# A transformer layer in eight batches: the row maxima of batch 1 move among batch 0's scores

## The chip, the cores and the metric

One core of a Trainium2 chip runs the whole kernel. Time is device time in microseconds of one launch. The engines work through queues of their own and wait for each other by semaphores: PE (TensorE, matmuls), ACT (ScalarE), DVE (VectorE), POOL (GpSimd) and SP (SyncE, whose queue issues the DMA transfers). ScalarE's queue can issue transfers too; in the kernel before only SP's does.

## What is computed

x is 8 x 256 x 256 (batch, token, feature), all in float32. Cut to what matters:

```python
# attention: 16 heads of 16, two query sets that share keys and values
scores = einsum('bhqd,bhkd->bhqk', q, k2) / sqrt(16); causal mask
p = softmax(scores); y = p @ v2
y = y1 - sigmoid(x @ Wlam) * y2
x = layernorm(x + y @ Wo)
# FFN: shared MLP of 1024, a routed MLP of 128 scaled by the top 2 of 8 logits
comb = sum of softmax(top2(x @ router.T))
x = layernorm(x + mlp(x, shared) + mlp(x, routed) * comb)
```

with `mlp(x) = (g * sigmoid(g) * u) @ down.T`, g = x @ gate.T and u = x @ up.T.

## The kernel before

Each batch of 256 tokens passes through four stages, and the stages of neighbouring batches are woven into each other by hand: every engine has its own list of instructions, written out in `iteration(i, ...)`, and an engine takes its list strictly in order.

**Projections.** float32 products are made of three fast passes (`product`, lines 666 to 668) of a high and a low part of each operand. `qk_job(b, n)`, n = 0 to 2, projects q and k of a batch into the PSUM banks ybank (12 matmuls). The result is cut into three bfloat16 parts: ScalarE copies it (`raw_part`, `first_part`), POOL subtracts (`rest_part`, L362), ScalarE copies (`second_part`), POOL subtracts (`third_part`, L388). SP stores the parts in DRAM (`store_part`, L256, nine per batch) and loads them back as stacks in which six products of parts lie on 96 rows (`load_stacks`, L272 and L274, twelve loads per batch; there are two stacks for each of q and k). xT is split by ScalarE (`split_xt`) and POOL (L356).

**Scores, twice.** First 22 units `s_unit(b, u)` (L724, L729) make the scores in the order in which a row maximum can be taken, in a ring of three PSUM banks; DVE reduces each (`row_max`, L1010), and a unit waits until the bank it takes was reduced. `max_job` transposes the maxima (L737), ScalarE and DVE make two bfloat16 rows of them (`max_first`, `max_second`), and SP loads these as two more rows of q's stack (`load_max`, L279). Then eight groups `t_group(b, g)` (L750, L754) make the scores again, transposed and with the maximum subtracted; ScalarE takes the exponentials (`exps`, L512, three per group), POOL masks (`causal`, L407), PE multiplies by v (`pv_group`, L778, two groups later), DVE evacuates (L1031).

**Output.** `y_jobs` (L791) transposes, DVE normalizes (`normalize_y`, L1042 to L1056), `yT_job` (L799) transposes back, `wo_job` projects into ybank, DVE adds the input (L1067) and takes the statistics.

**FFN.** `x1T_job`, router and logits, nine `gu_units` of 12 matmuls each with gate and up of 128 columns in two banks `ff` (ScalarE `gate_tanh` L520 and `h_first`, DVE `mlp_unit`, POOL `h_rests` L397), then the down products two iterations later.

In iteration i PE goes through: the 22 score units of batch i, with `qk_job(i + 1)` behind units 3, 6 and 10, the down products of batch i - 2, x1T, router and logits of batch i - 1 among them; gate/up unit 0; `max_job`; units 1 to 3; then the eight groups with units 4 to 6 among them; `y_jobs` with units 7 and 8; v of the next batch, `yT_job`, the first score unit of the next batch, `wo_job`. In iteration 0 there is no batch before it, so the scores stand alone but for batch 1's projections; in iteration 1 there are no down products yet.

SP's list in the set-up: xT of batch 0, the weights, nine stores, xT of batch 1, twelve stack loads. In an iteration: `load_x(i)`, nine stores of batch i + 1, xT of i + 2, `load_max(i)`, twelve stack loads of i + 1, in iteration 0 the three pieces of w_down.

Of the kernel before, what the change touches and what calls it, by code (L numbers as in the profile page):

```python
# [80 lines left out]
PROJ_CHUNKS = QK_JOBS + 1  # L81

# [15 lines left out]
def build_layer(nc, x, xT, w_proj, w_out, w_gu, w_down, w_router, out):  # L98
    with ExitStack() as ctx:
# [142 lines left out]

        block = ctx.enter_context(nc.Block())
# [3 lines left out]
        def _(sp):  # L247
# [15 lines left out]
            def load_stacks(b):  # L263
                if b >= STACKS:
                    sp.wait_ge(t_full, (b - STACKS + 1) * T_UNITS)
                for p in range(3):
                    sp.wait_ge(parts_stored[p], (b + 1) * (16 * QK_JOBS))
                    for s in range(SLOTS):

                        rows = slice(s, STACK_ROWS, SLOTS)  # L270
                        if Q_PARTS[s] == p:
                            sp.dma_start(q_stacks[b % STACKS][rows, :, :, :], scratch[p, :, :, 0:Q_JOBS, :]).then_inc(stack_loaded, 16)  # L272
                        if K_PARTS[s] == p:
                            sp.dma_start(k_stacks[b % STACKS][rows, :, :, :].rearrange("p r h t -> p r (h t)"), scratch[p, :, :, Q_JOBS, :]).then_inc(stack_loaded, 16)  # L274
# [17 lines left out]
            def iteration(i, has_next=True, has_last=True):  # L292
                load_x(i)
                if has_next:
                    store_parts(i + 1, range(QK_JOBS))
                if i + 2 < B:
                    load_xt(i + 2)
                load_max(i)
                if has_next:
                    load_stacks(i + 1)  # L300
# [29 lines left out]
        def _(pool):  # L330
# [90 lines left out]
            def iteration(i, has_next, has_prev, has_last):  # L421
# [11 lines left out]
                if has_prev:  # L433
                    h_rests(i - 1, range(FF_MAX[-1]))
                causal(i, range(0, 1))
                if has_prev:
                    h_rests(i - 1, FF_MAX[-1:])
                for g in range(1, GROUPS):
# [3 lines left out]
                    if has_prev and g - 1 in FF_SCORES:  # L442
                        n = FF_SCORES[g - 1]
                        h_rests(i - 1, range(n, n + 1))
                if has_prev:
# [24 lines left out]
        def _(act):  # L470
# [30 lines left out]
            def max_first(b):  # L501
# [3 lines left out]
                copy(max_parts[:, 0, :], misc[0:HEADS * Q_TILES, 0:P]).then_inc(max_h_done, 1)  # L505

# [66 lines left out]
            def iteration(i, has_next, has_prev, has_last):  # L573
                if has_next:
                    split_xt(i + 1)
# [11 lines left out]
                if has_prev:  # L587
                    x1T_first(i - 1)
                if has_next:
# [3 lines left out]
                if has_prev:  # L593
# [3 lines left out]
                if has_prev:  # L597
                    router_exp(i - 1)
                    mlp_units(i - 1, (FF_FIRST,))
                max_first(i)  # L600
                if has_prev:
# [3 lines left out]
                exps(i, 0)  # L605
                if has_prev:
                    h_first(i - 1, FF_MAX[-1])
                    gate_tanh(i - 1, FF_SCORES[0])
                for g in range(1, GROUPS):
# [53 lines left out]
        def _(pe):  # L663
# [48 lines left out]
            def s_unit(b, u):  # L712

                if u == 0:
# [6 lines left out]
                bank = ring[u % RING]  # L721
# [18 lines left out]
            def t_group(b, g):  # L740

                rows = slice(0, STACK_ROWS + MAX_PARTS)
                for u in range(3):
                    if g == 0:
# [71 lines left out]
            def x1T_job(b):  # L816
                pe.wait_ge(yT_lo_done, b + 1)
                for t in range(TT):
# [80 lines left out]
            def iteration(i, has_next, has_prev, has_last):  # L899
                if i == 2:  # L900
                    pe.wait_ge(mlp_w_lo_done, W_DOWN)
                if not has_prev:
                    first_scores(i)
                for u in range(S_UNITS):
                    if u > 0:
                        s_unit(i, u)
                    if has_next and u in QK_AT:
# [11 lines left out]
                if has_prev:  # L919
                    gu_units(i - 1, (FF_FIRST,))  # L920
                max_job(i, has_prev)
                if has_prev:
                    gu_units(i - 1, FF_MAX)
                pe.wait_ge(max_loaded, (i + 1) * (16 * MAX_PARTS))
                for g in range(GROUPS + 2):
                    if g < GROUPS:
                        t_group(i, g)
                    if g in FF_SCORES and has_prev:
                        gu_units(i - 1, (FF_SCORES[g],))
                    if g >= 2:  # L930
# [10 lines left out]
                if has_next:  # L941
                    v_job(i + 1, 1)
                    first_scores(i + 1)
                wo_job(i)

# [28 lines left out]
        def _(dve):  # L974
# [32 lines left out]
            def row_max(b, u):  # L1007
                dve.wait_ge(s_full, b * S_UNITS + u + 1)
                i, columns, keys = s_job(u)
                dve.tensor_reduce(neg_max[:, columns.start:columns.stop, i], ring[u % RING][:, 0:len(columns) * keys].rearrange("p (h k) -> p h k", k=keys),  # L1010
# [125 lines left out]
            def iteration(i, has_prev, has_last):  # L1136
# [9 lines left out]
                for u in range(1, S_UNITS):  # L1146
                    row_max(i, u)
                    if has_prev:

                        if u - 2 == X1T_AT:  # L1150
                            x1T_second(i - 1)
                        if u - 1 == LOGIT_AT:
                            router_top(i - 1, router_steps[0])
                if has_prev:
                    mlp_unit(i - 1, FF_FIRST)
                max_second(i)
                attn[0](dve.tensor_scalar(lam[:, :, :], lam_th[:, :, :], 0.5, 0.5, ALU.mult, ALU.add))
                if has_prev:
# [4 lines left out]
                if has_prev:  # L1163
                    mlp_unit(i - 1, FF_SCORES[0])
                for g in range(GROUPS):
                    if g == 0 and is_first(i):
                        dve.wait_ge(mlp_w_lo_done, W_GATE_UP)
                    if has_prev and g + 1 in FF_SCORES:
# [14 lines left out]
                if i + 1 < B:  # L1183
# [75 lines left out]
```

## Time and profile before

| | us |
|---|---|
| median of 3 runs | 481.44 (481.05 to 482.01) |
| the profiled execution | 480.8 |
| its span, first to last instruction | 479.1 |
| PE busy | 420.2 (88%) |
| DVE, ACT, POOL busy | 279.6, 237.2, 243.8 |
| mean granted clock of PE | 0.963 of full |

The profile shows one execution. Times in it count from the first instruction. An engine's busy time says nothing by itself of what it costs: what counts is which engine waits for which at each place. The granted clock has two levels here, 1.00 (2.4 GHz) and 0.50 (1.2 GHz). Matmuls are pipelined, so their starts are better marks than their ends: the distance between two starts is what a piece of PE's work takes.

### The profile page before, as it was taken

How to read it: one execution, taken by the hardware profiler on the slowest of the kernel's cores; microseconds unless marked ns; L12 is line 12 of the kernel's file. 1: busy time of each engine (PE TensorE's matmuls, PEld its weight loads, DVE VectorE, ACT ScalarE, POOL GpSimd, SP SyncE). 2: the span in 40 equal slices, each digit the busy share in tenths (PEclk: the TensorE clock that was granted, in tenths of full speed). 3: DMA queues.
4: the chain of work that ended last, by engine and by line, in shares of the span. 5: the costliest groups of instructions: out<-in, count | busy, mean ns of one | idle time of the engine just before them, and what ended most of it. 6: DMA issues, size and time to landing. Idle time of an engine off the chain costs nothing.

```text
span 479.1 us, 10336 instructions
## 1 busy us (share of the span) xinstructions
PE 420.2 (88%) x4008; PEld 336.0 (70%) x4008; DVE 279.6 (58%) x676; ACT 237.2 (50%) x532; POOL 243.8 (51%) x334
## 2 busy tenths in 40 slices
PE   5129687899999999999999999999999999997995
PEld 4126246775998579875988579866987588855995
DVE  3617237844758366745757476755757378746374
ACT  4604482477254843476254843475355831483140
POOL 8305374556354845567354834566364822383142
PEclk9659699999999999999999999999999999999899
DMA  8762760362023610381024511280034410000000
GB/s 287 233 150 69 201 176 1 113 169 64 1 77 105 142 45 24 99 191 36 23 80 125 118 45 38 87 199 24 23 91 115 98 47 0 4 1 24 1 23 23
DMA packets 34753, 40.41 MB, mean 84 GB/s; under 512 B 4240, under 2 KB 28304, under 8 KB 34448
## 3 DMA queue, kind: packets, MB, share of 16 engines
q1 hardware_dynamic: 34704, 39.75, 30.9%
q8 instruction: 32, 0.52, 0.5%
q14 instruction: 17, 0.14, 0.1%
HBM read 27.94 MB, written 11.53 MB: 82 GB/s over the span
## 4 chain that ended last, share of the span: by engine, by line
PE 66%; DVE 13%; ACT 10%; issue 4%; DMA 3%; SPq 2%; POOL 1%; POOLq 0%; DVEq 0%; ACTq 0%
PE ff L666 10%; PE ff L668 9%; PE ff L667 9%; PE ybank L778 8%; DVE neg_max L1010 7%; ACT prob L512 6%; PE ring L729 5%; PE ring L750 4%; PE ybank L666 4%; PE ybank L667 3%; PE ybank L668 3%; PE ybank L791 3%; PE ring L754 3%; PE ring L724 3%; DMA q_stack<-qk_parts_dram 2%
## 5 line engine op out<-in xcount | busy, mean ns | idle before, releaser
L1010 DVE TENSOR_REDUCE neg_max<-ring 128x2 f32<-128x512 f32 (+3 forms) x176 | 104.2, 636 | 46.2 <-PE ring L729 45.6
L512 ACT ACTIVATE prob<-ring 128x512 f32<-128x512 f32 x192 | 100.3, 620 | 14.7 <-PE ring L750 14.6
L397 POOL TENSOR_TENSOR h_lo<-h_full,h_hi 128x256 fp32r<-128x256 f32 x72 | 52.9, 734 | 100.2 <-ACT h_hi L472 100.2
L407 POOL TENSOR_SCALAR_AFFINE_SELECT prob<-prob 128x512 f32<-128x512 f32 x128 | 83.4, 676 | 23.8 <-ACT prob L512 23.5
L666 PE MATMUL ff<-x1T_hi,wg_lo 128*128 128x256 f32 x288 | 85.8, 298 | 0.1
L667 PE MATMUL ff<-x1T_lo,wg_hi 128*128 128x256 f32 x288 | 80.4, 279 | 0.0
L668 PE MATMUL ff<-x1T_hi,wg_hi 128*128 128x256 f32 x288 | 80.4, 279 | 0.0
L1031 DVE COPY yv<-ybank 128x256 f32<-128x256 f32 x64 | 26.5, 421 | 75.3 <-PE ybank L778 75.3
L520 ACT ACTIVATE gate_t<-ff 128x256 f32<-128x256 f32 x72 | 27.8, 386 | 73.9 <-PE ff L668 72.7
L724 PE MATMUL ring<-mask_b,ident_b 128*128 128x128 bf16 (+2 forms) x176 | 44.6, 254 | 20.6 <-DMA q_stack<-qk_parts_dram 18.4
L729 PE MATMUL ring<-k_stack,q_stack 96*128 96x256 bf16 (+3 forms) x512 | 58.9, 235 | 0.0
L666 PEld LDWEIGHTS ff<-x1T_hi,wg_lo 128*128 128x128 f32 x288 | 54.3, 188 | 3.6 <-DVE h_full L1026 1.9
L778 PE MATMUL ybank<-prob,v_ones 128*32 128x256 f32 (+1 forms) x1024 | 54.9, 336 | 0.1
L667 PEld LDWEIGHTS ff<-x1T_lo,wg_hi 128*128 128x128 f32 x288 | 54.3, 188 | 0.0
L668 PEld LDWEIGHTS ff<-x1T_hi,wg_hi 128*128 128x128 f32 x288 | 54.0, 188 | 0.0
L750 PE MATMUL ring<-q_stack,k_stack 98*128 98x512 bf16 x128 | 41.8, 399 | 7.7 <-ACT prob L512 3.9
L1020 DVE SCALAR_TENSOR_TENSOR gate_t<-gate_t,ff 128x256 f32<-128x256 f32 x72 | 29.9, 415 | 26.3 <-ACT gate_t L520 26.2
L778 PEld LDWEIGHTS ybank<-prob,v_ones 128*32 128x32 f32 x1024 | 26.9, 110 | 24.5 <-DVE yv L1031 5.7
L362 POOL TENSOR_TENSOR rest<-rest,parts 128x512 f32<-128x512 f32 x21 | 24.4, 1161 | 31.5 <-ACT parts L472 31.5
L472 ACT ACTIVATE rest<-ybank 128x512 f32<-128x512 f32 x21 | 12.5, 594 | 53.1 <-PE ybank L668 53.1
L729 PEld LDWEIGHTS ring<-k_stack,q_stack 96*128 96x128 bf16 x512 | 36.6, 100 | 3.0 <-issue 0.6
L666 PE MATMUL ff<-wd_hi,h_lo 128*128 128x256 f32 x124 | 37.7, 304 | 0.0
(164 smaller groups left out, 886.1 us busy)
## 6 DMA issues: line engine op xcount, KB each, us to landing
q_stack<-qk_parts_dram SPq DMA_DIRECT2D x48, 256.0 KB, 4.6
qk_parts_dram<-parts SPq DMA_DIRECT2D x72, 128.0 KB
k_stack<-qk_parts_dram SPq DMA_DIRECT2D x48, 128.0 KB, 4.4
xt_raw<-xT SPq DMA_DIRECT2D x8, 256.0 KB, 2.7
xz<-x SPq DMA_DIRECT2D x8, 256.0 KB, 2.8
out<-xz SPq DMA_DIRECT2D x7, 256.0 KB, 2.2
prob<-w_gu SPq DMA_DIRECT2D x1, 1152.0 KB, 7.8
yv<-w_gu SPq DMA_DIRECT2D x1, 1024.0 KB, 9.5
```

The costliest lines, as they stand in the source:

```text
L397: pool.tensor_tensor(h_lo[:, n, :], h_full[:, n % RING, :], h_hi[:, n, :].bitcast(F32), ALU.subtract).then_inc(h_lo_done, 1)
L407: pool.affine_select(out=v, in_=v, compare_op=ALU.is_ge, fill=0.0, base=0, pattern=[[0, 2], [HALF, 2], [0, 2], [1, HALF]], channel_multipl ...
L512: act.activation(prob[:, g % RING, u, :], ring[u][:, :], ACT.Exp, scale=SCALE).then_inc(exp_done, 1)
L666: pe.matmul(o, lhs_lo, rhs_hi, start=first, stop=False)
L667: pe.matmul(o, lhs_hi, rhs_lo, start=False, stop=False)
L668: return pe.matmul(o, lhs_hi, rhs_hi, start=False, stop=last)
L724: pe.matmul(o[:, :, keys - HALF:keys], ident_b[:, :], mask_b[:, :].unsqueeze(1).to_broadcast([P, len(columns), HALF]), start=True, stop=Fa ...
L729: mm = pe.matmul(o[:, j, :], q_stacks[b % STACKS][rows, row, block, i * P:(i + 1) * P], k_stacks[b % STACKS][rows, row, block, 0:keys], st ...
L750: mm = pe.matmul(ring[u][:, :], keys_of(b, rows, n, slice(0, P)), q_pair(b, rows, n, slice(0, 2 * T)), start=True, stop=True)
L778: mm = pe.matmul(bank[V_COLS * j:V_COLS * (j + 1), t * P:T], v_ones[:, t, 2 * g + j // 2, :], p, start=(t == 0), stop=(t == TT - 1))
L1010: dve.tensor_reduce(neg_max[:, columns.start:columns.stop, i], ring[u % RING][:, 0:len(columns) * keys].rearrange("p (h k) -> p h k", k=keys),
L1020: dve.scalar_tensor_tensor(gate_t[:, n % RING, :], gate_t[:, n % RING, :], 1.0, ff[n % 2][:, 0:T], ALU.add, ALU.mult).then_inc(gate_done, 1)
```

## The change

Batch 1 is singled out (`EARLY = 1`).

- Set-up: xT of batch 1 is loaded and split ahead of the stores and of the other weights' splits. ScalarE's queue issues the six stack loads of part 0 of batch 0 behind the values' copies, SP's the other six.
- Iteration 0: PE does the three `qk_job` of batch 1 ahead of batch 0's score units and none among them. SP waits for batch 0's stacks before it stores batch 1's parts. The two rows of batch 0's maxima are loaded by ScalarE's queue (`load_first_max`). From step 2 of the group loop on, three score units of batch 1 stand in each step behind `t_group` and ahead of `pv_group`, in the two banks `ff` in place of the ring, and DVE reduces them there; `max_job(1)` follows `wo_job(0)`.
- Iteration 1: PE begins with the three `qk_job` of batch 2, then goes to the groups. x1T, router, logits and gate/up units 0 to 6 of batch 0 stand in steps 1, 2, 3 and 3 to 9. ScalarE's first instruction is `max_first(1)`, ahead of the split of xT; SP loads the maxima ahead of the stores. POOL's masks come ahead of batch 0's `h_rests`.

The diff, cut to its core:

```diff
+EARLY = 1
+EARLY_FROM, EARLY_STEP = 2, 3
+EARLY_X1T, EARLY_ROUTER, EARLY_LOGIT = 1, 2, 3
...
+        def s_bank(b, u):
+            return ff[u % 2] if b == EARLY else ring[u % RING]
+        def early_units(step):
+            first = max(step - EARLY_FROM, 0) * EARLY_STEP
+            return range(first, min(first + EARLY_STEP, S_UNITS) if step >= EARLY_FROM else first)
...  SP, iteration
+                if i == EARLY:
+                    load_max(i)
+                if is_first(i):
+                    sp.wait_ge(stack_loaded, 16 * STACK_LOADS)
                 if has_next:
                     store_parts(i + 1, range(QK_JOBS))
...
-                load_max(i)
+                if i not in (0, EARLY):
+                    load_max(i)
...  SP, set-up
+            load_xt(1)
             for n, p in ((0, 0), (1, 0), (0, 1), (2, 0), (1, 1), (2, 1), (0, 2), (1, 2), (2, 2)):
                 store_part(0, n, p)
-            load_xt(1)
-            load_stacks(0)
+            load_stacks(0, range(1, 3))
...  ScalarE, set-up
             for t in range(TT):
                 values(0, t)
+            load_part(act, 0, 0)
+            split_xt(1)
             split_weight(wo_hi[:, :, :], wo_raw, wo_loaded)
...  ScalarE, iteration
+                if i == EARLY:
+                    max_first(i)
                 if has_next:
-                    split_xt(i + 1)
+                    if has_prev:
+                        split_xt(i + 1)
                     raw_part(i + 1, 0)
...
+                if is_first(i):
+                    load_first_max()
...
+                if i == EARLY:
+                    for step in range(1, GROUPS + 2):
+                        if step < GROUPS:
+                            exps(i, step)
+                        if step == EARLY_X1T:
+                            x1T_first(i - 1)
+                        if step == EARLY_ROUTER:
+                            router(i - 1)
+                        if step >= EARLY_LOGIT:
+                            gate_tanh(i - 1, step - EARLY_LOGIT)
+                        if step == EARLY_LOGIT:
+                            router_exp(i - 1)
+                        if step > EARLY_LOGIT:
+                            h_first(i - 1, step - EARLY_LOGIT - 1)
...  PE, s_unit
+                if b == EARLY:
+                    if u > 1:
+                        pe.wait_ge(max_done, b * S_UNITS + u - 1)
...  PE, iteration
                 if not has_prev:
+                    for n in range(QK_JOBS):
+                        qk_job(i + 1, n)
                     first_scores(i)
+                if i == EARLY:
+                    for n in range(QK_JOBS):
+                        qk_job(i + 1, n)
...
                     if g < GROUPS:
                         t_group(i, g)
+                    if i == EARLY:
+                        if g == EARLY_X1T:
+                            x1T_job(i - 1)
+                        if g == EARLY_ROUTER:
+                            router_job(i - 1)
+                        if g == EARLY_LOGIT:
+                            logit_job(i - 1)
+                        if g >= EARLY_LOGIT:
+                            gu_units(i - 1, (g - EARLY_LOGIT,))
...
+                    if i + 1 == EARLY:
+                        if g == EARLY_FROM:
+                            first_scores(i + 1)
+                        for u in early_units(g):
+                            if u > 0:
+                                s_unit(i + 1, u)
                     if g >= 2:
                         pv_group(i, g - 2, has_next)
...
                 wo_job(i)
+                if i + 1 == EARLY:
+                    max_job(i + 1, False)
...  DVE, iteration
                 for g in range(GROUPS):
+                    if i == EARLY:
+                        step = g + 2
+                        if step == EARLY_ROUTER:
+                            x1T_second(i - 1)
+                        if step == EARLY_LOGIT:
+                            router_top(i - 1, router_steps[0])
+                        if step >= EARLY_LOGIT:
+                            mlp_unit(i - 1, step - EARLY_LOGIT)
+                        if step == EARLY_LOGIT + 1:
+                            router_sum(i - 1, *router_steps)
+                    if i + 1 == EARLY:
+                        for u in early_units(g + 2):
+                            row_max(i + 1, u)
...
                     evacuate_pv(i, g)
```

## Rows read from the trace of the kernel before

**Rows 1.** The page's slices: busy tenths of TensorE (PE) in 40 slices.

```profile
PE   5129687899999999999999999999999999997995
```

**Rows 2.** SP's queue in order of time: start us, us, engine line, transfer, count.

```profile
9.23 8.27 SPq L256 DMA_DIRECT2D qk_parts_dram<-parts  x9
...
18.07 0.64 SPq L272 DMA_DIRECT2D q_stack<-qk_parts_dram  x1
...
25.16 0.60 SPq L272 DMA_DIRECT2D q_stack<-qk_parts_dram  x1
...
50.35 1.16 SPq L279 DMA_DIRECT2D q_stack<-max_parts  x2
```

**Rows 3.** Line 272 (stack loads), 0 to 70 us: from issue to landing.

```profile
DMA to landing us min/median/max: 3.4/5.0/7.6
```

**Rows 4.** Line 279 (the maxima's two rows), whole span: from issue to landing.

```profile
DMA to landing us min/median/max: 2.1/2.1/2.2
```

**Rows 5.** Windows: stretch, length, engines' busy time, granted clock, DMA share, GB/s.

```profile
24.00:26.00 2.00, 0.00 (x0) 0.00 (x0) 0.00 (x0) 0.00 (x0) 1.14 (x1) 0.50 1.07 237
...
50.00:52.00 2.00, 0.01 (x1) 0.00 (x0) 0.37 (x2) 0.27 (x1) 0.00 (x0) 0.69 0.65 197
...
61.00:62.00 1.00, 1.00 (x16) 0.43 (x8) 0.42 (x1) 0.30 (x2) 1.00 (x2) 1.00 1.14 264
```

**Rows 6.** Groups of instructions, 33 to 50 us, DVE: busy us, mean ns, idle before.

```profile
L1010 DVE TENSOR_REDUCE neg_max<-ring 128x2 f32<-128x384 f32 (+3 forms) x22 | 12.6, 636 | 13.3 <-PE ring L729 13.3
```

**Rows 7.** PE in order of time, columns as in rows 2, idle before in brackets.

```profile
53.12 1.04 PE L750 MATMUL ring<-q_stack,k_stack 98*128 98x512 bf16 x2 [3.11 <-DMA q_stack<-max_parts]
...
69.46 1.34 PE L791 MATMUL ybank<-ident,yv 128*128 128x128 f32 x8
...
80.89 0.37 PE L666 MATMUL ybank<-xt_hi,wp_lo 128*128 128x256 f32 x1
...
85.23 0.23 PE L724 MATMUL ring<-mask_b,ident_b 128*128 128x128 bf16 x1
...
86.28 0.23 PE L724 MATMUL ring<-mask_b,ident_b 128*128 128x128 bf16 x1 [0.20 <-DVE neg_max L1010]
...
101.57 0.36 PE L666 MATMUL ff<-x1T_hi,wg_lo 128*128 128x256 f32 x1
...
103.07 0.60 PE L750 MATMUL ring<-q_stack,k_stack 98*128 98x512 bf16 x2
...
107.17 0.86 PE L778 MATMUL ybank<-prob,v_ones 128*32 128x256 f32 x16
107.96 0.60 PE L750 MATMUL ring<-q_stack,k_stack 98*128 98x512 bf16 x2
...
108.71 0.86 PE L778 MATMUL ybank<-prob,v_ones 128*32 128x256 f32 x16
...
120.16 0.36 PE L666 MATMUL ff<-x1T_hi,wg_lo 128*128 128x256 f32 x1
```

**Rows 8.** ScalarE (ACT) in order of time.

```profile
61.82 6.35 ACT L512 ACTIVATE prob<-ring 128x512 f32<-128x512 f32 x12 [0.70 <-PE ring L750]
...
82.61 0.60 ACT L472 ACTIVATE rest<-ybank 128x512 f32<-128x512 f32 x1 [3.97 <-PE ybank L668]
...
89.61 0.60 ACT L472 ACTIVATE x1T_hi<-misc 128x512 fp32r<-128x512 f32 x1
```

**Rows 9.** GpSimd (POOL) in order of time.

```profile
72.56 1.85 POOL L392 TENSOR_TENSOR wd_lo<-h_full,wd_hi 128x768 fp32r<-128x768 f32 x1
78.72 1.29 POOL L356 TENSOR_TENSOR xt_lo<-xt_raw,xt_hi 128x512 fp32r<-128x512 f32 x1 [4.31 <-ACT xt_hi L472]
```

**Rows 10.** VectorE (DVE) in order of time.

```profile
71.13 1.50 DVE L1046 TENSOR_TENSOR recip<-recip,lam 128x16 f32<-128x16 f32 x1
...
79.98 0.69 DVE L1067 TENSOR_TENSOR xz<-ybank,xz 128x512 f32<-128x512 f32 x1 [1.15 <-PE ybank L668]
...
120.73 0.17 DVE L1046 TENSOR_TENSOR recip<-recip,lam 128x16 f32<-128x16 f32 x1
```

More of the change, by code:

```diff
@@ L241, in qk_bank, with load_part @@
             return (ybank[0], ybank[1], misc if is_first(b) else ybank[0])[n]
+        def load_part(queue, b, p):
+            queue.wait_ge(parts_stored[p], (b + 1) * (16 * QK_JOBS))
+            for s in range(SLOTS):
+                rows = slice(s, STACK_ROWS, SLOTS)
+                if Q_PARTS[s] == p:
+                    queue.dma_start(q_stacks[b % STACKS][rows, :, :, :], scratch[p, :, :, 0:Q_JOBS, :]).then_inc(stack_loaded, 16)
+                if K_PARTS[s] == p:
+                    queue.dma_start(k_stacks[b % STACKS][rows, :, :, :].rearrange("p r h t -> p r (h t)"), scratch[p, :, :, Q_JOBS, :]).then_inc(stack_loaded, 16)
+        def s_bank(b, u):
[3 more added lines that the diff above has]
+            return range(first, min(first + EARLY_STEP, S_UNITS) if step >= EARLY_FROM else first)
         block = ctx.enter_context(nc.Block())
@@ L261, in store_parts, with load_stacks @@
                         store_part(b, n, p)
-            def load_stacks(b):
+            def load_stacks(b, parts):
                 if b >= STACKS:
                     sp.wait_ge(t_full, (b - STACKS + 1) * T_UNITS)
[L266 to L274, printed above, removed]
+                for p in parts:
+                    load_part(sp, b, p)
             def load_max(b):
@@ L604, in iteration @@
                     act.wait_ge(mlp_w_lo_done, 1)
-                exps(i, 0)
-                if has_prev:
+                if i == EARLY:
[12 more added lines that the diff above has]
+                            h_first(i - 1, step - EARLY_LOGIT - 1)
+                    h_first(i - 1, FF_Y0 - 1)
+                else:
+                    exps(i, 0)
+                if has_prev and i != EARLY:
                     h_first(i - 1, FF_MAX[-1])
                     gate_tanh(i - 1, FF_SCORES[0])
-                for g in range(1, GROUPS):
+                for g in range(1, GROUPS if i != EARLY else 1):
                     exps(i, g)
@@ L902, in iteration @@
                 if not has_prev:
+                    for n in range(QK_JOBS):
+                        qk_job(i + 1, n)
                     first_scores(i)
[L904 removed]
+                if i == EARLY:
+                    for n in range(QK_JOBS):
+                        qk_job(i + 1, n)
+                for u in range(S_UNITS if i != EARLY else 0):
                     if u > 0:
                         s_unit(i, u)
[L907 removed]
+                    if has_next and has_prev and u in QK_AT:
                         qk_job(i + 1, QK_AT.index(u))
@@ L1009, in row_max @@
                 i, columns, keys = s_job(u)
-                dve.tensor_reduce(neg_max[:, columns.start:columns.stop, i], ring[u % RING][:, 0:len(columns) * keys].rearrange("p (h k) -> p h k", k=keys),
+                dve.tensor_reduce(neg_max[:, columns.start:columns.stop, i], s_bank(b, u)[:, 0:len(columns) * keys].rearrange("p (h k) -> p h k", k=keys),
                                   AX_X, ALU.max,
```

86 lines of the change are left out of this document (57 added, 29 removed).

## Prediction

> **What bounds the kernel now.** I read the page's slices first, then the chain of waits, then the windows and the order of time of each engine over the first 130 us. TensorE (PE) works in nine tenths or more of most slices after the first six [rows 1]: from batch 2 on it is the bound, and what the change can gain lies before. There PE waits for others four times. (a) It stands still until 32.87 us for the q and k stacks of batch 0: SP's queue stores the parts, then issues twelve loads from 18.07 us, the last at 25.16 us [rows 2], and that one lands after 7.6 us [rows 3]; while it does, the DMA engines are full (share 1.07) and PE's granted clock is 0.50, its lower level of 1.2 GHz [rows 5]. (b) Batch 0's scores for the maxima need 22 reductions on VectorE (DVE), 12.6 us of work [rows 6]; with projections between them the stage lasts from 32.87 to about 49.7 us. (c) The maxima's own rows take 2.1 us to land [rows 4], PE waits 3.11 us for them [rows 7], and the clock falls to 0.50 again, not to rise before 61 us [rows 5]. (d) Batch 1's scores for the maxima run from 79.8 to 96 us, again at DVE's pace, with projections, x1T, router and the first gate/up unit between them. W below is the end of batch 0's output projection, 79.8 us (DVE's addition follows at 79.98 [rows 10]).
>
> **The start.** ScalarE's queue now issues six of the twelve loads. At 0.64 us each (twelve from 18.07 to 25.8 us [rows 2]) that moves SP's last issue from 25.2 to about 20.8 us; batch 1's xT load leaves the place ahead of it as well. Bounds for the last landing: issue plus the median 5.0 us, 25.8 us; or no gain from the second queue at all, since the engines are already full at 24 us, and only the xT load is saved, 32 us. Twelve loads are 2.36 MB, at the 237 GB/s of that window 10 us, and they can't start before the third of the first parts is stored (the fourth of nine stores that run from 9.23 to 17.5 us [rows 2], behind the weights; I estimate 16 to 16.5 us), and bytes flow some 2 us later (the 2.1 us of the smallest load [rows 4]). I take 29.4 us, nearer to 20.8 + 7.6 = 28.4 than to 32. That is -3.5 us. The Trainium skill (DMA: Bandwidth & Descriptors, section "Issuing engines are not separate DMA queues") says that a second issuing engine saves only the issuing time, as all end on the same 16 DMA engines; the full share in the row agrees, and by it alone the gain would be nearer the small bound. ScalarE pays for it: six issues, 3.8 us if they cost what SP's do, bounds 0 and 7. Behind them stand the split of batch 1's xT and those of the weights, 5.1 us in a row, so batch 1's first copy comes at about 25.5 to 26.5 us. PE does batch 1's three projections, about 1.5 us each at 2.4 GHz (twice that at 1.2), while it would wait anyway; the third may end at 28 us, or 29.4 at the lower clock. That cover is full: nothing added.
>
> **Batch 0's scores (b).** Without projections between them the stage is DVE's 12.6 us plus 0.6 us in front, 13.2 instead of 16.8 us: -3.6, together -7.1 us.
>
> **Its maxima (c).** They go out on ScalarE's queue, because SP's is full: it now waits for batch 0's stacks, stores batch 1's parts (the chain of copies and subtractions took 10.5 us before, so it ends near 37 us) and then issues the twelve loads of batch 1, 37 to 45 us, landing by about 50. So the two small rows, at 43 us, travel beside full engines, which no row shows; alone they land in 2.1 us [rows 4], loads in such a crowd in up to 7.6 us [rows 3]. I take 3.1: they are small and on a queue of their own. +1.0 us, at most +5.5. The same page ("Queues, rings and completion order") says that a DMA engine takes turns between queues, packet by packet; by that the delay would be near 0 and the sum 1 us lower; no row here has two queues. T(0), the stage of batch 0's own scores (L750, L754) and their products with v (L778), starts at 47.0 instead of 53.12 us.
>
> **T(0) with batch 1's maxima in it.** Now 53.12 to 69.46 us, 16.3 us [rows 7]. In each of eight steps PE gets three more score units, in the two FFN banks. With two banks the third unit has to wait until DVE has reduced the first. Rows: with three banks, a unit at 85.23 us frees its bank for the one at 86.28 [rows 7], so 1.05 us from a unit to the next of its bank, for 384 columns; for 512 the reduction is 0.16 us longer. With the third unit's own 0.24 to 0.33 us a triple takes about 1.3 (three of them) or 1.55 us (four), and the last step has one unit, 0.3: 10.4 us. Scores of a group take 0.75 us, products 0.79 [rows 7]. The first three groups take 4.4 us, as now. T(0) = 4.4 + 10.4 + 5 x 0.75 + 8 x 0.79 = 24.9 us. The clock: now it is back 7.9 us after T(0)'s start; in the stretch from 4.4 to 7.9 us PE's own work is at half speed, +1.4 us (0 if it never falls). So 26.3 us, +9.9 us. ScalarE (three exponentials, 1.6 us a step [rows 8]), DVE (2.3) and POOL (1.3) stay under PE's 3.0 us. Batch 1's stacks are needed after the third group, 51.4 us; they land at about 50.
>
> **To W.** VectorE's L1046 took 1.50 us at 71.13 us, 0.17 us in the next batch, and waited until POOL's splits of w_down were through [rows 9, 10]. With T(0) longer, ScalarE's exponentials end 5 us before PE's last products, and those splits end at about 1.2 us behind T(0), before L1046 (1.7 us behind it). Saved: about 1.8 us (bounds 0 and 2.2). W is at -7.1 + 1.0 + 9.9 - 1.8 = +2.0 us.
>
> **From W to batch 0's gate/up unit 7** (120.16 us now, W + 40.4 [rows 7]). The 16 us stage (d) is gone, but what stood beside it isn't, and now has no cover. ScalarE first waits for the transposed maxima (W + 0.6), then splits xT of batch 2 (before W until now), POOL subtracts, 1.3 us [rows 9], and PE's projection starts at W + 2.6. 1.7 us later comes the first copy, and the copies and subtractions take 7.0 us until ScalarE is free (82.61 to 89.61 us [rows 8]): exponentials of batch 1 start only at W + 11.35, though its maxima have landed at W + 4.6. PE is idle for about 4 us. Then exponentials (1.6), a copy (0.55), exponentials (1.6), x1T's two parts and hand-overs (1.5): W + 16.4; router 0.7, products 0.8: W + 17.9. Steps 3 to 7 are PE's: 0.75 + 1.5 (a gate/up unit, 101.57 to 103.07 us [rows 7]) + 0.79 = 3.04, with 0.2 for the logits 15.4: W + 33.3. Two steps without scores, 4.6: W + 37.9. DVE does unit 6 ahead of the last evacuation, so the second transposes end at W + 39.6. Idle for 4 us, PE loses its clock before the exponentials, as it did behind (b): half speed costs the router and the first products 0.7 + 0.8 us, of which I take 1.2 (bounds 0 and 3). 40.8 against 40.4: +0.4 us. Behind that nothing is changed and PE is the bound.
>
> **The sum**, against the profiled execution's own 480.8 us: -3.5 - 3.6 + 1.0 + 9.9 - 1.8 + 0.4 = +2.4, 483.2 us. The median of the runs lies 0.6 us above that execution: 483.8 us.
>
> **Rivals.** (1) The long stages pack better: loads land at 28 us (-1.4), the small rows lose nothing (-1.0), the clock holds in T(0) and behind W (-2.6), triples overlap more than the bank rule says (-1.5). Together -6.5 at most, any half of it is -3.2: 477.3 to 480.5 us, typically 479.5. For it: PE is idle less than before in the first 45 us, and busy early. (2) Slower by a wait for batch 1's stacks. PE takes its queue in order, so if they land after the third group (51.4 us; my margin is 1.4 us) scores, products and exponentials all stand. Landing at 7.6 us from the last issue, with ScalarE's six issues at 1.2 us instead of 0.64: 45.5 + 3.4 + 7.6 = 56.5 us, +5 us: 489 us. It decides from 51.4 us on. For it: the engines are full in each burst of loads; against: in the second burst the median was under 5 us. (3) It doesn't do what it says at the start: transfers and not issues are the bound, S(0) begins at 32 us: +2.6, 486.5 us. (4) The two changes in T(0) and behind W are dearer than thought, DVE's reductions lagging: +3, 487 us.
>
> **Chances.** Forecast 0.45 (481 to 486), rival 1 0.28, rival 2 0.11, rival 3 0.08, rival 4 0.08. A measurement of this kernel can tell about 0.2%, 1 us. Faster than 480.5 us: rival 1 and a little of the forecast's lower end, 0.30; within: 0.20; slower: 0.50. The range, 477.5 to 489 us, leaves out a tenth on each side.
>
> **What would show it.** First score unit (L724) at 29.4 us; the 22 reductions without a gap over 0.2 us and the transposed maxima at 42.6 us; the small rows' landing under 3.5 us; T(0) of 26 us with PE waiting for neg_max once in each step; L1046 at 0.2 us; exponentials of batch 1 at W + 11; PE idle for 4 us ahead of them with a clock of 0.50. Wrong would be a wait of PE for q_stack in T(0), steps of 2.5 us or less, or exponentials of batch 1 at W + 5.

## The result, and the profile after

The changed kernel takes 488.51 us (median of 4 runs, 486.60 to 491.42), the one before 481.50 us (4 runs on the same chip): 1.6% slower, ratio 1.016, 95% interval 1.0135 to 1.0184. The forecast was 483.8 us, slower by 2.4 us; it is slower by 7.0 us. The profiled execution is the fastest of the four: 486.6 us, its span 484.8 us. Medians below are of all runs of a kernel, but the ratios leave out runs over 1.5% above its fastest (four of e4's ten, five of e8's).

First the page of the changed kernel: busy tenths of PE, its granted clock and the DMA engines' share, in 40 slices of 12.1 us.

```profile
PE   4285787689999999999999999999999999999895
...
PEclk9785599879999999999999999999999999999998
DMA  8778700175003700254112810362122610000000
```

In the first ten slices, where the kernel before had 5129687899 [rows 1], PE's digits have only moved: the third is 8 in place of 2, the fourth 5 in place of 9, and both rows add up to 64. The clock has a second dip at the eighth and ninth slices, around 97 us, where there was none.

PE in order of time in the changed kernel, at the marks that the prediction named: start us, us, engine line, operation, out<-in, shape and count; in brackets PE's idle time before it, and what ended it.

```profile
31.68 0.39 PE L784 MATMUL ring<-mask_b,ident_b 128*128 128x512 bf16 x1 [1.42 <-DMA q_stack<-qk_parts_dram]
...
44.58 0.42 PE L797 MATMUL misc<-ident,neg_max 128*64 128x128 f32 x1 [1.07 <-DVE neg_max L1101]
51.42 1.03 PE L815 MATMUL ring<-q_stack,k_stack 98*128 98x512 bf16 x2 [6.42 <-DMA q_stack<-max_parts]
...
61.19 0.28 PE L784 MATMUL ff<-mask_b,ident_b 128*128 128x256 bf16 x1 [0.45 <-DVE neg_max L1101]
...
77.56 1.33 PE L856 MATMUL ybank<-ident,yv 128*128 128x128 f32 x8
...
86.03 0.27 PE L797 MATMUL misc<-ident,neg_max 128*64 128x128 f32 x1
88.57 0.36 PE L723 MATMUL ybank<-xt_hi,wp_lo 128*128 128x256 f32 x1 [2.27 <-POOL xt_lo L376]
...
98.42 0.88 PE L815 MATMUL ring<-q_stack,k_stack 98*128 98x512 bf16 x2 [3.17 <-ACT prob L543]
...
127.57 0.36 PE L723 MATMUL ff<-x1T_hi,wg_lo 128*128 128x256 f32 x1
```

They answer to [rows 7], and give the sum term by term (us; "before" from [rows 7] and the first waits told there):

| stage | before | forecast | after |
|---|---|---|---|
| first score unit of batch 0 (L784, before L724) | 32.87 | 29.4 | 31.68 |
| scores for the maxima, to their transposition | 16.84 | 13.2 | 12.90 |
| from there to T(0), the rows of maxima | 3.41 | 4.4 | 6.84 |
| T(0) | 16.34 | 26.3 | 26.14 |
| from T(0) to W | 10.33 | 8.5 | 8.47 |
| from W to gate/up unit 7 of batch 0 | 40.37 | 40.8 | 41.54 |
| gate/up unit 7 | 120.16 | 122.6 | 127.57 |

W is 86.03 us, where the transposed maxima of batch 1 follow the output projection. Of the 7.4 us at unit 7, 5.7 are left at the end of the span. The stretch from 440 to 450 us in the kernel before, then in the changed one (length, busy time of PE, PE's weight loads, DVE, ACT, POOL, then granted clock, DMA share, GB/s):

```profile
440.00:450.00 10.00, 7.98 (x54) 7.56 (x53) 3.75 (x10) 2.68 (x6) 2.73 (x6) 0.83 0.00 0
440.00:450.00 10.00, 7.52 (x89) 6.06 (x82) 7.79 (x22) 2.53 (x7) 2.78 (x5) 1.00 0.09 29
```

The traces of all kernels here are of one of these two kinds. From unit 7 to the end they take either 357.2 to 357.5 us, with a clock of 1.00 from 430 to 460 us (changed, e1, e3, e10, e12), or 358.8 to 359.2 us, with a fall of the clock in that stretch (before, e2, e4, e5, e6, e8, e9, e11). One trace each doesn't show what decides between them, but a single traced execution can differ from another by these 1.7 us behind everything that the change touches.

The DMA side, in three views of the changed kernel. ScalarE's queue and ScalarE in order of time:

```profile
17.83 0.64 ACTq L254 DMA_DIRECT2D q_stack<-qk_parts_dram  x1
...
45.34 1.17 ACTq L536 DMA_DIRECT2D q_stack<-max_parts  x2
...
97.77 1.57 ACT L543 ACTIVATE prob<-ring 128x512 f32<-128x512 f32 x3
```

The two rows of maxima (line 536), from issue to landing:

```profile
DMA to landing us min/median/max: 5.1/5.3/5.5
```

And windows, as in [rows 5]: stretch, length, busy time of PE, PE's weight loads, DVE, ACT, POOL, then granted clock, DMA share, GB/s.

```profile
26.00:28.00 2.00, 2.00 (x11) 2.00 (x11) 2.00 (x2) 2.00 (x4) 0.00 (x0) 0.50 1.08 234
46.00:48.00 2.00, 0.00 (x0) 0.00 (x0) 0.00 (x0) 0.00 (x0) 0.00 (x0) 0.50 1.13 241
90.00:92.00 2.00, 2.00 (x11) 2.00 (x11) 0.00 (x0) 1.08 (x2) 0.09 (x1) 0.50 0.00 0
96.00:98.00 2.00, 0.00 (x0) 0.00 (x0) 0.00 (x0) 1.72 (x4) 1.20 (x2) 1.00 0.42 128
...
104.00:106.00 2.00, 2.00 (x19) 0.81 (x19) 0.12 (x1) 0.37 (x1) 1.06 (x2) 0.50 1.03 268
108.00:110.00 2.00, 2.00 (x26) 1.26 (x25) 0.75 (x2) 0.57 (x3) 0.85 (x2) 1.00 1.13 240
```

ScalarE's loads begin at 17.83 us, when the first parts have landed. From 22 to 30 us the DMA engines are full (1.08 at 26 us), as before the change [rows 5]: the same loads take the same time, whoever issues them. And at 46 us, while the rows of maxima travel, the engines are full again with batch 1's stack loads (1.13): the rows need 5.3 us in place of 2.1 [rows 4], and PE does nothing. The last four windows are for the clock, below: behind W it is 0.50 twice, from about 89.5 to 93 us, behind the wait of 2.27 us at 88.57 us, and from about 100 to 106.5 us.

### The profile page after: what moved, and what is told of

It is laid out like the page before. It is cut to its first block, busy times and chain, and to the rows that moved or that the text cites. A ratio compares the mean times of both kernels' runs of the same rounds, so it can differ in the third digit from the quotient of the medians.

```text
span 484.8 us, 10334 instructions
## 1 busy us (share of the span) xinstructions
PE 425.0 (88%) x4008; PEld 338.9 (70%) x4008; DVE 279.7 (58%) x676; ACT 237.6 (49%) x532; POOL 245.6 (51%) x334
## 4 chain that ended last, share of the span: by engine, by line
PE 64%; DVE 14%; ACT 11%; DMA 5%; issue 4%; POOL 2%; SPq 0%; POOLq 0%; ACTq 0%; DVEq 0%
PE ff L723 10%; PE ff L725 9%; PE ff L724 9%; DVE neg_max L1101 8%; ACT prob L543 7%; PE ybank L843 7%; PE ring L789 4%; PE ring L815 4%; PE ybank L723 3%; PE ybank L856 3%; PE ybank L724 3%; PE ybank L725 3%; PE ring L819 3%; PE ring L784 2%; DMA q_stack<-qk_parts_dram 2%
## 5 line engine op out<-in xcount | busy, mean ns | idle before, releaser
L1101 DVE TENSOR_REDUCE neg_max<-ring 128x2 f32<-128x384 f32 (+3 forms) x154 | 91.0, 636 | 32.2 <-PE ring L789 31.7
L724 PE MATMUL ff<-x1T_lo,wg_hi 128*128 128x256 f32 x288 | 80.2, 278 | 0.0
L724 PEld LDWEIGHTS ff<-x1T_lo,wg_hi 128*128 128x128 f32 x288 | 54.3, 188 | 0.0
L789 PE MATMUL ring<-k_stack,q_stack 96*128 96x64 bf16 (+3 forms) x448 | 52.8, 238 | 0.0
L723 PE MATMUL ybank<-xt_hi,wp_lo 128*128 128x256 f32 x92 | 30.0, 326 | 17.3 <-issue 8.5
L784 PE MATMUL ring<-mask_b,ident_b 128*128 128x128 bf16 (+2 forms) x154 | 39.1, 254 | 2.6 <-DMA q_stack<-qk_parts_dram 1.4
L408 POOL TENSOR_TENSOR parts<-rest,parts 128x512 bf16<-128x512 f32 x24 | 27.8, 1162 | 19.6 <-ACT parts L498 11.6
L382 POOL TENSOR_TENSOR rest<-rest,parts 128x512 f32<-128x512 f32 x21 | 25.8, 1230 | 23.2 <-ACT parts L498 23.2
```

What stands on the lines that cost most here:

```text
L723: pe.matmul(o, lhs_lo, rhs_hi, start=first, stop=False)
L724: pe.matmul(o, lhs_hi, rhs_lo, start=False, stop=False)
L784: pe.matmul(o[:, :, keys - HALF:keys], ident_b[:, :], mask_b[:, :].unsqueeze(1).to_broadcast([P, len(columns), HALF]), start=True, stop=Fa ...
L789: mm = pe.matmul(o[:, j, :], q_stacks[b % STACKS][rows, row, block, i * P:(i + 1) * P], k_stacks[b % STACKS][rows, row, block, 0:keys], st ...
```

## The experiments

e1 to e12 differ from the changed kernel or from an earlier experiment by the edit shown, in diffs cut to their core. Times are medians; each ratio is to the kernel before, run in turns on the same chip, with its 95% interval. The stages are read from the profile of each kernel as in the table above.

### e1: not woven

```diff
-EARLY = 1
+EARLY = -1
```

> The changed kernel with EARLY = -1: batch 1's maxima and its gate/up units stand where they stood before the change; the rest of the change stays (six stack loads on ScalarE's queue, batch 1's xT and projections early, batch 0's maxima rows on ScalarE's queue). My theory: weaving batch 1's scores into T(0) costs more than the stage behind W gives back, because PE was nearly full in that stage (3.8 of 4 us from 80 to 88 us). Before, the scores cost nothing there; woven, T(0) takes 26.1 instead of 16.3 us, and W to gate/up unit 7 takes 41.5 instead of 40.4 us. So without the weaving T(0) starts near 51.4 us as in the changed kernel, takes 16.3 us again, and the kernel is about 1.5 us faster than before the change, 480 us. Rival: the start is at fault (ScalarE's issues, late rows) and the weaving pays; then this kernel stays slow, 484 us or more.

Measured: 478.14 us, ratio 0.9941 (0.9919 to 0.9963). PE in e1, in order of time:

```profile
51.91 1.03 PE L815 MATMUL ring<-q_stack,k_stack 98*128 98x512 bf16 x2 [7.06 <-DMA q_stack<-max_parts]
...
67.97 1.34 PE L856 MATMUL ybank<-ident,yv 128*128 128x128 f32 x8
```

T(0) is 16.06 us again, and W to unit 7 is 40.37 us, as before. So the rest of the change gains 2.7 us (the kernel before took 480.86 us in the same turns), and the weaving costs some 10 us (0.9941 against 1.016, 2.2%). The rows of maxima are late here too (PE waits 7.06 us). The profiled execution is the slowest of e1's ten (479.75 us), and its way from T(0) to W is 12.16 us, with a clock of 0.50 from about 73 to 80 us; in e11, whose code is the same there, it is 10.33 us at 1.00. So in this trace nothing is gained yet at unit 7 (120.50 us), and the changed kernel is only 7.1 us behind it there; in e11 unit 7 starts at 114.80 us, 5.4 us ahead of the kernel before.

### e2: the rows of maxima ahead of batch 1's stack loads

e1, with this edit:

```diff
-                if i not in (0, EARLY):
+                if i != EARLY:
                     load_max(i)
...
-                if is_first(i):
-                    load_first_max()
```

> As e1, and batch 0's two rows of maxima are issued by SP's queue again, ahead of the twelve stack loads of batch 1, which so begin some 5 us later. My theory: the rows landed 5.3 us from their issue instead of 2.1 because the DMA engines were full of batch 1's stack loads. Here they land in 2.1 to 2.2 us, T(0) starts 3 us earlier than in e1 (48.2 us), and the kernel takes 477 us. Rival: ScalarE's queue itself is slow, or the delay has another cause (the core's clock, the rows' place): then either the landing stays at 5 us or the time doesn't follow, 480 us.

Measured: 475.37 us, ratio 0.9874 (0.9833 to 0.9915). PE in e2:

```profile
48.31 1.03 PE L813 MATMUL ring<-q_stack,k_stack 98*128 98x512 bf16 x2 [3.09 <-DMA q_stack<-max_parts]
...
63.97 1.33 PE L854 MATMUL ybank<-ident,yv 128*128 128x128 f32 x8
```

and its line 294, all sixteen rows of maxima, from issue to landing:

```profile
DMA to landing us min/median/max: 2.1/2.1/2.1
```

The rows land in 2.1 us and T(0) starts 3.6 us earlier than in e1, at 48.31 us; the time follows by 2.8 us.

### e3: batch 1's stack loads wait for the rows

The changed kernel, woven (as e4 and e5 are), with this edit:

```diff
+                if is_first(i):
+                    sp.wait_ge(max_loaded, 16 * MAX_PARTS)
                 if has_next:
                     load_stacks(i + 1, range(3))
```

> The changed kernel; SP's queue holds the twelve stack loads of batch 1 back until batch 0's rows of maxima have landed. The rows stay on ScalarE's queue. If crowding is the cause, they land in 2.1 us and T(0) starts at 48 us; if ScalarE's queue is the cause, 5 us as before. The stacks then come too late for the first woven score unit: loads from 48 to 56 us, landing at 60 to 62 us, so PE waits some 8 us for q_stack in T(0), and the kernel takes about 491 us.

Measured: 492.58 us, one run. Line 538, the rows on ScalarE's queue, from issue to landing, and then the waits of PE for DMAs from 48 to 70 us:

```profile
DMA to landing us min/median/max: 2.1/2.1/2.2
```

```profile
48.77 1.04 PE L817 MATMUL ring<-q_stack,k_stack 98*128 98x512 bf16 x2 [3.12 <-DMA q_stack<-max_parts]
61.19 0.61 PE L786 MATMUL ff<-mask_b,ident_b 128*128 128x512 bf16 x1 [8.01 <-DMA q_stack<-qk_parts_dram]
```

ScalarE's queue isn't slow: with nearly empty DMA engines (share 0.02 from 44 to 50 us) it delivers in 2.1 us. It is the crowd. The second line shows what rival 2 of the prediction would have been: 8.0 us of PE's time, when the woven units stand in its queue ahead of their stacks. In the changed kernel itself no such wait was there (T(0) went on at 55.6 us without one), so rival 2 didn't come.

### e4: three banks

```diff
-                    if u > 1:
-                        pe.wait_ge(max_done, b * S_UNITS + u - 1)
+                    if u > 2:
+                        pe.wait_ge(max_done, b * S_UNITS + u - 2)
...
-            return ff[u % 2] if b == EARLY else ring[u % RING]
+            return (ff[0], ff[1], misc)[u % 3] if b == EARLY else ring[u % RING]
```

> The changed kernel with three PSUM banks for batch 1's woven score units instead of two. My theory: in seven steps PE waits 0.43 to 0.51 us for the reduction of the first unit of the triple, because the third takes its bank. With a third bank that wait goes, and the first unit of the next step has been reduced long ago: T(0) 22.8 to 23.2 us instead of 26.1, the kernel about 3 us faster than the changed one. Rival: DVE or ScalarE becomes the bound of a step; then T(0) stays over 25 us.

Measured: 486.99 us (ten runs, 480.76 to 489.18), ratio 1.0083 (1.0044 to 1.0122). PE in e4:

```profile
50.49 1.03 PE L815 MATMUL ring<-q_stack,k_stack 98*128 98x512 bf16 x2 [5.61 <-DMA q_stack<-max_parts]
...
72.94 0.63 PE L856 MATMUL ybank<-ident,yv 128*128 128x128 f32 x4
```

T(0) is 22.45 us: 3.7 us shorter than the changed kernel's 26.14, so the waits for the bank are real. But the kernel gains little: its median lies 6.1 us above the kernel before in the same turns, the changed one's 7.0. In the traced run the way to W takes 0.8 us more (9.28), and from W (82.2 us) to unit 7 it takes 44.5 us instead of 41.5. Windows of e4 behind its W:

```profile
92.00:94.00 2.00, 0.00 (x0) 0.00 (x0) 0.00 (x0) 1.51 (x4) 1.20 (x3) 1.00 0.39 104
96.00:98.00 2.00, 2.00 (x9) 1.19 (x8) 0.00 (x0) 2.00 (x5) 1.20 (x2) 0.50 0.43 131
...
102.00:104.00 2.00, 2.00 (x16) 0.63 (x8) 0.42 (x1) 0.70 (x2) 0.00 (x0) 0.50 0.93 235
106.00:108.00 2.00, 2.00 (x15) 1.39 (x17) 0.26 (x1) 0.48 (x2) 0.00 (x0) 0.50 1.09 269
```

PE's clock is 0.50 from about 95 to 108.5 us, twice as long as in the changed kernel (about 100 to 106.5 us), and falls at the end of a wait of 3.9 us. Both have the earlier fall too (here from 85 to 88 us, behind the wait for the split of xT). In this run most of the gain in T(0) went into the longer second fall.

### e5: batch 2's xT split ahead of the copy of the maxima

```diff
-                if i == EARLY:
-                    max_first(i)
                 if has_next:
                     if has_prev:
                         split_xt(i + 1)
+                    if i == EARLY:
+                        max_first(i)
```

> The changed kernel; in iteration 1 ScalarE splits batch 2's xT ahead of the copy of batch 1's transposed maxima, while it idles behind the values' copies. My theory: behind W the chain maxima copy, xT split, POOL's subtraction sets when batch 2's first projection starts (2.6 us behind W), and with it all copies ahead of batch 1's exponentials. Now the split is done 2 us earlier, the projection starts 0.9 us behind W when the addition is through, and W to gate/up unit 7 falls from 41.5 to 39.9 us: the kernel 1.6 us faster than the changed one, 487 us. Rival: the maxima's landing sets the stage; then nothing is gained.

Measured: 487.49 us (four runs, 483.82 to 489.52), ratio 1.0114 (1.0056 to 1.0172). W to unit 7 is 39.18 us, 2.4 less than in the changed kernel. Batch 2's first projection starts at W + 1.0 instead of W + 2.5, the first fall of the clock is gone (1.00 until 97 us), batch 1's exponentials start at W + 9.7 instead of W + 11.7, and PE's clock is back at 1.00 at about 104.5 us, W + 17.8, where the changed kernel's is at about 106.5 us, W + 20.5. So the order on ScalarE is late by what was expected of it or a little more, since the clock changes too; the two aren't told apart here. The whole kernel's 1.0 us is less than its own scatter.

### e8: three banks, and the gap filled

e4, with this edit:

```diff
+            def filler(n):
+                for h in range(2):
+                    f = slice((2 * n + h) * P, (2 * n + h + 1) * P)
+                    for k in range(DK):
+                        product(ff[1][:, h * T:(h + 1) * T], wp_hi[:, k, f], wp_lo[:, k, f],
+                                xt_hi[:, k, :], xt_lo[:, k, :], k == 0, k == DK - 1)
...
                     if i == EARLY:
+                        if g == 0:
+                            for n in range(2):
+                                filler(n)
```

> As e4 (three banks), with two projection-sized jobs of 12 matmuls each, whose results nobody reads, on PE behind batch 1's first group of scores, in a bank that is free: 3 us of work in a gap in which PE waited 3.9 us for batch 1's first exponentials. My theory: e4's gain in T(0), 3.7 us, is given back behind W because PE's clock falls to half in and behind that gap (from 94.8 to 108.4 us in e4's trace), not because of the wait itself. With the gap filled the clock stays up, W to gate/up unit 7 takes 40 us instead of 44.5, the kernel takes 483 us, and its runs scatter less than e4's 8 us. Rival: the late exponentials cost the time; then extra work on PE changes nothing or costs up to 1 us.

Measured: 487.07 us (ten runs, 480.33 to 489.54), ratio 1.0047 (1.0002 to 1.0092); W to unit 7 44.51 us in the profiled execution, which is the slowest of the ten (489.54 us). A miss: neither the median nor the scatter changed. Windows of e8:

```profile
94.00:96.00 2.00, 2.00 (x19) 1.95 (x17) 0.00 (x0) 1.49 (x4) 1.19 (x2) 1.00 0.41 128
96.00:98.00 2.00, 1.07 (x6) 0.32 (x5) 0.00 (x0) 1.98 (x5) 1.79 (x2) 1.00 0.41 121
98.00:100.00 2.00, 1.50 (x9) 0.68 (x8) 0.00 (x0) 2.00 (x5) 1.40 (x2) 1.00 0.46 137
100.00:102.00 2.00, 1.13 (x5) 0.88 (x6) 0.69 (x1) 1.87 (x4) 2.00 (x4) 0.67 0.51 137
102.00:104.00 2.00, 2.00 (x20) 1.15 (x19) 0.00 (x0) 0.37 (x1) 1.53 (x3) 0.50 1.02 300
...
106.00:108.00 2.00, 2.00 (x9) 2.00 (x10) 0.64 (x3) 0.44 (x1) 1.30 (x2) 0.50 1.09 237
```

The gap is full (PE busy 2.00 of 2 us at 94 us), yet the clock falls in the window of 100 us, behind 4.5 us in which PE is busy for half to three quarters of the time and never idle for 1 us on end. "The idle gap drops the clock" was too simple. The runs of e8 also differ: the two fastest (480.33 and 480.62 us) have a mean granted clock of 0.972 over the whole kernel, the five slowest 0.949 to 0.952.

### e9: woven, all three mends

e8 with e5's order on ScalarE.

> The woven kernel with all three mends: three banks, the gap filled, the xT split early. If weaving is a loss in itself, because PE had little to gain in the stage that it empties, this is still slower than the same kernel not woven (e1, 478.1 us): T(0) 22.5 instead of 16.3 us, W to gate/up unit 7 38.5 instead of 40.4 us, so 4 us above e1, 482 us. Rival: with the mends the weaving pays, and the time is under 478 us.

Measured: 484.24 us (ten runs, 480.85 to 486.61), ratio 1.0050 (1.0017 to 1.0082). T(0) 22.51, W to unit 7 41.50 us: 3 us more than expected, again with a clock of 0.50 for ten us. As expected it is slower than e1. Windows of e9:

```profile
92.00:94.00 2.00, 0.97 (x4) 0.37 (x5) 0.00 (x0) 1.99 (x5) 1.73 (x2) 1.00 0.40 117
94.00:96.00 2.00, 1.61 (x9) 0.70 (x8) 0.00 (x0) 2.00 (x5) 1.46 (x2) 0.82 0.46 137
96.00:98.00 2.00, 1.35 (x7) 0.90 (x7) 0.69 (x1) 1.81 (x4) 2.00 (x4) 0.50 0.53 144
```

This execution (484.72 us) is in the middle of its ten, and the fall at 95.4 us follows a thinly filled stretch as in e8; ahead of it lies one wait of 1.30 us.

### e10: the thin stretch filled too

e9, with this edit:

```diff
                         if g == EARLY_X1T:
                             x1T_job(i - 1)
+                            filler(0)
                         if g == EARLY_ROUTER:
+                            filler(1, 1)
                             router_job(i - 1)
```

The second number is how many of the two halves are done.

> As e9, with more unread matmuls: twelve behind x1T's transposes and six ahead of the router. In e8's trace the gap ahead of the exponentials was filled (PE waited 0.7 instead of 3.9 us), and the clock fell all the same, at 100.9 us, in the stretch that follows, where PE waits for exponentials and x1T and is busy for 0.3 to 0.9 of each us. So my theory changes: the thinly filled stretch from W + 11 to W + 17 lets the clock fall, not the gap alone. With that stretch filled too the clock stays at 1.00 until the gate/up units, W to gate/up unit 7 takes 38.5 to 39 us instead of e9's 41.5, and the kernel takes 481.5 us. Rival: the clock isn't what costs; then nothing changes or the extra work adds up to 1 us. In either case a kernel that stays above e1 (478.1 us), though its clock holds, shows that the weaving is a loss in itself.

Measured: 481.78 us (ten runs, 480.79 to 483.42), ratio 1.0026 (1.0009 to 1.0042). Windows of e10, W at 84.7 us:

```profile
92.00:94.00 2.00, 1.79 (x16) 1.58 (x14) 0.00 (x0) 1.49 (x4) 1.19 (x2) 1.00 0.42 121
94.00:96.00 2.00, 0.78 (x2) 0.19 (x2) 0.00 (x0) 2.00 (x5) 1.98 (x2) 1.00 0.43 133
96.00:98.00 2.00, 1.94 (x17) 1.93 (x18) 0.00 (x0) 1.99 (x6) 1.21 (x2) 1.00 0.45 136
98.00:100.00 2.00, 2.00 (x17) 1.71 (x16) 0.69 (x1) 2.00 (x5) 2.00 (x4) 1.00 0.43 114
100.00:102.00 2.00, 2.00 (x26) 1.05 (x24) 0.43 (x1) 0.99 (x3) 1.74 (x3) 1.00 0.96 296
102.00:104.00 2.00, 2.00 (x22) 1.76 (x26) 0.41 (x3) 1.31 (x4) 1.30 (x2) 1.00 0.91 242
104.00:106.00 2.00, 2.00 (x28) 1.47 (x21) 1.18 (x3) 1.37 (x5) 0.00 (x1) 1.00 1.04 238
```

The clock stays at 1.00, W to unit 7 is 37.88 us, the shortest of all, and the runs scatter by 2.6 us where e4's and e8's scattered by 8 and 9 and e9's by 5.8. PE's wait of 1.30 us is there as in e9; what differs is the stretch behind it. Eighteen matmuls more than in e9 (42 in all), whose results nobody reads, save 3.6 us against its 41.5. So the clock is what costs behind W in the traced runs. That it makes the scatter is likely but not shown run by run: e10's ten (480.79 to 483.42) lie where the fastest of e4, e8 and e9 do (480.76, 480.33, 480.85), so the filling makes no fast run faster, it takes the long ones away. For the kernel as a whole the gain over e9 is not clear of noise, as the intervals of the ratios overlap.

### e11 and e12: who issues batch 0's stack loads

e11 is e2 again. e12 (first run as e6) is e2 with all twelve loads on SP's queue:

```diff
-            load_part(act, 0, 0)
...
-            load_stacks(0, range(1, 3))
+            load_stacks(0, range(3))
```

> As e2 (not woven, the rows ahead of the stack loads), with all twelve stack loads of batch 0 issued by SP's queue again; batch 1's xT and projections stay early. My first theory was that issuing is the bound of the start; the trace of the changed kernel shows full DMA engines from 22 to 30 us and a first score unit at 31.7 us, so now I expect transfers to be the bound: the first unit moves by 0.7 us at most (32.5 us) and the kernel takes 475.4 to 476.2 us. Rival (issuing is the bound): the first unit at 34 us or later, 478 us.

> e2 again, in more rounds and on the same chip as e12: 475.4 us, a ratio of 0.987 to the kernel before. It tells, with e12, whether six loads on ScalarE's queue gain anything.

> e6 again. If transfers are the bound of the start, it agrees with e11 within 1 us; if issuing were, it would be 2 us slower or more.

Measured: e6 476.94 us, ratio 0.9889 (0.9842 to 0.9936); then, six runs each on one chip, e11 475.17 us, 0.9878 (0.9857 to 0.9899), and e12 475.36 us, 0.9887 (0.9863 to 0.9911). The first score unit in e11 and in e12:

```profile
31.67 0.39 PE L782 MATMUL ring<-mask_b,ident_b 128*128 128x512 bf16 x1 [1.25 <-DMA q_stack<-qk_parts_dram]
```

```profile
31.32 0.61 PE L781 MATMUL ring<-mask_b,ident_b 128*128 128x512 bf16 x1 [6.42 <-DMA q_stack<-qk_parts_dram]
```

Six loads on a second queue gain nothing: the first unit comes even 0.35 us earlier with all of them on SP's. But PE waits 6.42 us there, as batch 1's projections are through earlier, and the scores begin at a clock of 0.50: they take 13.73 instead of 12.91 us, and T(0) starts at 48.56 against 47.96 us. The two kernels end within 0.2 us of each other. e11 is also the version to keep: it is 1.2% faster than the kernel before and 2.7% faster than the changed one.

## Why the prediction was wrong, point by point

**Direction, and most terms, right.** Four of six terms came within 0.7 us: batch 0's scores without projections (12.90, forecast 13.2 us), T(0) with the woven units (26.14, 26.3 us), the way to W with POOL's splits out of the way (8.47, 8.5 us; L1137, before L1046, took 0.17 us), W to unit 7 (41.54, 40.8 us). The bank rule's waits are in the trace, 0.43 to 0.51 us in six steps. That the stage behind W would give back nothing was the argument that the change is slower; e1 bears it out. (The sum behind W has a slip: its terms to the router add up to W + 16.6, not W + 16.4.)

**The start was mis-sized: 1.2 us instead of 3.5.** I put the first unit at 29.4 us, near the bound that comes from issuing. The row with a DMA share of 1.07 stood in my own groups; by it the bound was 32 us, and rival 3 was the case. The rule of the Trainium skill that I set aside (DMA: Bandwidth & Descriptors, "Issuing engines are not separate DMA queues") is borne out by e11 against e12: no difference. What the start does gain, it gains by the earlier xT and projections, not by the second queue.

**The rows of maxima were mis-sized: +3.4 us instead of +1.0.** The bounds 0 and 5.5 were right, the choice between them was not. "Small, and on a queue of their own" was no argument from a row. e2 and e3 take the crowd away, on either queue, and the rows land in 2.1 us again. The same page's rule that a DMA engine takes turns between the queues packet by packet ("Queues, rings and completion order") was read as a delay near 0; measured were 3.8 to 6.1 us to land, in the woven kernels and in e1, so that reading fails here, and the measurement decides. Why the rows were held up, by turns or otherwise, isn't shown.

**The clock behind W** was taken as 1.2 us, for one fall ahead of the exponentials. In the profiled execution the stage came out 0.7 us over the forecast, but the mechanism was in part another: the gap was there (3.17 us, exponentials at W + 11.7), the clock fell only behind it, at about 99.7 us, and an earlier fall, behind the wait of 2.27 us after W, was not foreseen. That the total agrees is partly luck. It isn't one value either: W to unit 7 was 41.5, 41.5 and 44.5 us in the changed kernel, e3 and e4, which have the same order of work there, and 37.9 with the clock held (e10, with e5's order). The median lies 1.9 us above the profiled execution, the fastest run of four. A fall of the clock in the stretch from 440 to 450 us, which the profiled execution was spared, would account for 1.7 of them; the recorded mean clocks of the other three runs (0.953 to 0.956 against 0.955) don't decide it, and only one run has a trace.

The sum: 2.4 forecast + 2.3 (start) - 0.3 + 2.4 (rows) - 0.2 + 0.7 = 7.3 us at unit 7; measured 7.4. The start and the rows of maxima are 4.7 us of the 5.0 that were missing: these two terms failed, and both for the same reason, the full DMA engines.

**What the weaving costs.** T(0), the way to W and W to unit 7 together: before 67.0 us, changed 76.2, e10 70.4 (e11, not woven, 66.8). Even with a third bank, the better order and the clock held, it is 3.4 us more than before: T(0) takes 6.9 us more, and what follows gives back only 3.5. The unread matmuls stand behind W, so the 6.9 us are free of them; whether they cost something of what is given back isn't shown. The stage that the weaving empties, in windows of the kernel before:

```profile
80.00:84.00 4.00, 3.85 (x46) 3.40 (x45) 3.93 (x9) 1.08 (x2) 1.46 (x6) 1.00 0.00 0
84.00:88.00 4.00, 3.80 (x37) 3.50 (x37) 3.12 (x7) 2.58 (x5) 3.19 (x3) 1.00 0.25 70
88.00:92.00 4.00, 2.92 (x29) 2.33 (x29) 3.34 (x6) 2.73 (x6) 2.39 (x4) 1.00 0.41 117
92.00:96.00 4.00, 3.62 (x32) 2.63 (x29) 3.81 (x10) 0.57 (x2) 1.11 (x1) 1.00 0.57 169
```

PE is busy for 14.19 of these 16 us, DVE for 14.20: the stage was as full for PE as for DVE, and emptying it of DVE's work frees at most the 1.8 us in which PE idled. In T(0) PE was busy for 15.76 of the 16 us from 53 to 69 us, so each woven unit there is added to PE's time.

## What to carry to other kernels

A stage that seems to run at one engine's pace is worth emptying only if the others idle in it: add up PE's share in the very stretch before moving work out, and ask what will cover the chains that ran beside it. A small load on the critical path belongs ahead of the large ones, in time and not only on another queue; and where the DMA engines are full, don't count on a second issuing engine: here it gained nothing.

## What the runs showed of the hardware

- Two loads of 16 KB land in 2.1 us alone, whichever queue issues them (e2, e3), and in 3.8 to 6.1 us while the DMA engines are full (share 1.05 to 1.09 from 45 to 50 us in e1, e4 and the changed kernel).
- PE's clock fell in e8 without an idle stretch of 1 us ahead of it, behind 4.5 us at half to three quarters busy, and in e9 behind a similar stretch with one wait of 1.30 us; with that stretch filled it stayed up (e10), in one trace each. It cost 3.6 us in e9 (41.5 against 37.9 us). In e4 and e8 the stage took 6.6 us more than in e10, which holds ScalarE's order too (2.4 us between e5 and the changed kernel, part of it again the clock).
